# One transposing DMA for each moved unit, unit 24 moved, and two column sums on VectorE, in a graph layer kernel on one core

## The reference

```
h  = relu(layernorm(x));  support = act_quant(relu(act_quant(h) @ weight_quant(weight)))
x  = x + adj @ support                       # layer 0
h  = relu(layernorm(x))
S  = (adj + adj.T) / 2 + I;  d = rowsum(S) ** -0.5
x  = x + (adj @ (d[:, None] * S * d[None, :])) @ h    # layer 1
```

## Time and profile before

| | |
|---|---|
| median of 3 runs | 495.47 us (495.06 to 495.62) |
| the profiled execution's own time | 496.49 us |
| its span, first to last instruction | 494.7 us |
| TensorE busy | 478.1 us, 97% of the span |
| TensorE clock granted | 1.000 of full |
| transposing DMAs | 42, one for each half (high, low) of 21 moved units |

### The profile page before, as it was taken

How to read it: one execution, slowest core, us unless ns; L and a number is a source line. 1 busy time by engine, 2 the same in 40 slices (tenths; PEclk the granted TensorE clock), 3 DMA queues, 4 the chain that set the end, 5 groups by cost and what they waited for, 6 DMA issues and landing times.

```text
span 494.7 us, 6414 instructions
## 1 busy us (share of the span) xinstructions
PE 478.1 (97%) x2358; PEld 232.0 (47%) x2358; DVE 268.5 (54%) x360; ACT 154.1 (31%) x300; POOL 46.6 (9%) x54
## 2 busy tenths in 40 slices
PE   1899999999999999999999999999999999999997
PEld 1755544444454444444444444444444444444446
DVE  4966996779999688876997767340100001000010
ACT  1787833767562435344521121140000000000000
POOL 2320963213200000000000000000000000000000
PEclk9999999999999999999999999999999999999999
DMA  8986999999986242332232321045010000100001
GB/s 286 401 333 161 233 193 231 225 220 229 233 241 249 65 135 98 95 117 85 85 122 91 113 99 42 0 168 193 23 42 21 21 21 21 42 21 21 21 23 43
DMA packets 63180, 62.66 MB, mean 127 GB/s; under 512 B 46136, under 2 KB 46392, under 8 KB 63160
## 3 DMA queue, kind: packets, MB, share of 16 engines
q1 hardware_dynamic: 63152, 62.40, 44.3%
q10 hardware_dynamic: 8, 0.00, 0.0%
HBM read 42.99 MB, written 8.39 MB: 104 GB/s over the span
## 4 chain that ended last, share of the span: by engine, by line
PE 84%; DVE 8%; DMA 4%; SPq 2%; ACT 1%; issue 1%; POOL 0%; ACTq 0%
PE ps_a L1204 31%; PE ps_p L1102 13%; PE ps_p L1167 7%; PE ps_a L1167 7%; PE ps_b L1167 7%; PE ps_m L1167 4%; PE ps_h L1167 4%; DMA feat<-in_x 2%; PE ps_b L1053 1%; PE ps_m L1102 1%; PE ps_h L1102 1%; DVE at L763 1%; DVE small L944 1%; PE ps_b L1220 1%; PE ps_a L1220 1%; PE ps_a L1053 1%
## 5 line engine op out<-in xcount | busy, mean ns | idle before, releaser
L1102 PE MATMUL ps_p<-small,at 128*128 128x512 f16 x448 | 99.2, 379 | 0.4 <-DVE feat L884 0.4
L1022 DVE SCALAR_TENSOR_TENSOR feat<-ps_a,feat 128x512 f32<-128x512 f32 (+1 forms) x16 | 10.8, 675 | 148.7 <-PE ps_a L1204 144.2
L1204 PE MATMUL ps_a<-small,at 128*128 128x512 f16 x360 | 80.2, 379 | 0.0
L1204 PE MATMUL ps_a<-a_in,at 128*128 128x512 f16 x360 | 80.2, 379 | 0.0
L1102 PEld LDWEIGHTS ps_p<-small,at 128*128 128x128 f16 x448 | 43.7, 98 | 50.8 <-DVE feat L884 0.7
L584 ACT ACTIVATE split<-a_in 128x1024 f16<-128x1024 f32 x30 | 31.7, 1057 | 101.8 <-PE ps_p L1167 90.0
L940 DVE TENSOR_TENSOR split<-a_in,split 128x1024 f16<-128x1024 f32 x30 | 36.7, 1224 | 34.0 <-ACT split L584 34.0
L1204 PEld LDWEIGHTS ps_a<-small,at 128*128 (+1 forms) x360 | 35.2, 98 | 42.5
L1204 PEld LDWEIGHTS ps_a<-a_in,at 128*128 (+1 forms) x360 | 35.2, 98 | 42.5
L1167 PE MATMUL ps_p<-feat,split 128*128 (+1 forms) x180 | 43.9, 379 | 0.5 <-DVE small L944 0.5
L1167 PE MATMUL ps_a<-feat,split 128*128 (+1 forms) x180 | 43.8, 379 | 0.0
(11 more groups left out here) (182 smaller groups left out, 436.0 us busy)
## 6 DMA issues: line engine op xcount, KB each, us to landing
a_in<-in_adj SPq DMA_DIRECT2D x46, 512.0 KB, 3.9
at<-in_adj SPq DMA_DIRECT2D x16, 512.0 KB, 8.9
out<-feat SPq DMA_DIRECT2D x31, 256.0 KB, 4.3
feat<-in_x SPq DMA_DIRECT2D x8, 512.0 KB, 11.6
feat<-out SPq DMA_DIRECT2D x4, 1024.0 KB, 9.3
at<-in_L_gnn_weight SPq DMA_DIRECT2D x2, 512.0 KB, 4.0
at<-at SPq DMA_TRANSPOSE x42, 4.7
split<-in_adj SPq DMA_DIRECT2D x1, 512.0 KB, 15.7
```

Source lines behind the costliest of these rows:

```text
L1022: nc.vector.scalar_tensor_tensor(out, products, 1.0 / (SA * SZ), out, ALU.mult, ALU.add).then_inc(y_out, 1)
L1102: last = nc.tensor.matmul(l0_bank(r), at_block(r, lo, j), small[:, j * D:(j + 1) * D], start=(j == 0 and lo == 0), stop=(j == T - 1 and lo ...
L1204: last = nc.tensor.matmul(BANK[n], at_block(t, lo, j), z_part(j, z_lo), start=(j == 0 and lo + z_lo == 0), stop=(j == T - 1 and lo == 1))
```

## The change

- `EVEN` gets unit 24: it is no longer turned by TensorE but moved. Round 10 turns nothing; round 9 moves 23, 24 and 25.
- A moved unit is one transposing DMA of 128 x 2048 in place of two of 128 x 1024, and it starts when the low part is ready. For that `at` is laid out unit by unit: a unit's high and low halves are neighbours. There is one semaphore for each staging buffer.
- Since the halves of units 28 to 31 now lie elsewhere over the staging buffers, `hi_turned(28)` waits for unit 26 alone, `hi_turned(30)` for none, and `hi_turned(31)` for unit 29.
- The column sums of units 10 and 14 move from ScalarE to VectorE, at the ends of rounds 5 and 7; those of 18 to 26 stand in other rounds on ScalarE.
- The load of 28 is started behind the move of 24, that of 29 behind the move of 25 (before: both behind 25, 29 first).

```diff
-EVEN = (10, 12, 14, 18, 20, 22, 26)
+EVEN = (10, 12, 14, 18, 20, 22, 24, 26)
+SUMMED_LATE = (10, 14)
...
+        def staged(u):
+            k = stage_no(u)
+            return late(14 + k // 2, 2 * W * (k % 2 if k < 2 else 1), 2 * W, f16)
         def stage(u, lo):
+            return staged(u)[:, lo * W:(lo + 1) * W]
...
+        def at_half(u, lo):
+            return at[:, (2 * u + lo) * W:(2 * u + lo + 1) * W]
         def at_block(r, lo, j):
-            return at[:, ds(r * PAIR + lo * N + j * P, P)]
+            return at[:, ds(r * PAIR + j // B * 2 * W + lo * W + j % B * P, P)]
...
-                 9: [23, 25], 10: [26], 11: [27, 29]}
+                 9: [23, 24, 25], 10: [26], 11: [27, 29]}
-        SUMS_OF = {5: [[(10, FIRST)], [], [(10, LAST)]], 7: [[(12, FIRST)], [(12, LAST)], []],
-                   8: [[(14, FIRST)], [(14, LAST)], []], 9: [[(18, FIRST)], [(18, LAST)], []],
-                   10: [[], [], [(20, FIRST)]], 11: [[], [(20, LAST)], [(22, FIRST)]],
-                   12: [[], [], [(22, LAST), (26, FIRST)]], 13: [[], [], [(26, LAST)]]}
+        SUMS_OF = {7: [[(12, FIRST)], [(12, LAST)], []], 8: [[(18, FIRST)], [(18, LAST)], []],
+                   9: [[(20, FIRST)], [(20, LAST)], []], 10: [[(22, FIRST)], [], [(22, LAST)]],
+                   11: [[], [], [(24, FIRST), (24, LAST)]], 12: [[], [], [(26, FIRST), (26, LAST)]]}
...
             def move(u):
-                for lo, ready in ((0, hi_ready), (1, lo_ready)):
-                    sp.wait_ge(ready, MOVED.index(u) + 1)
-                    if u == 29:
-                        wait_moved(sp, MOVED[-3])
-                        wait_moved(sp, MOVED[-2])
-                    elif u >= 12:
-                        free_slot(waited_in(u)[lo])
-                    sp.dma_start_transpose(at_half(u // 2, lo, u % 2).rearrange("p (b i) -> p b i", i=P), stage(u, lo))\
-                      .then_inc(at_moved[stage_no(u)][lo], 16)
+                sp.wait_ge(lo_ready, MOVED.index(u) + 1)
+                if u == 29:
+                    wait_moved(sp, MOVED[-2])
+                elif u >= 12:
+                    free_slot(waited_in(u)[u % 2])
+                sp.dma_start_transpose(at_unit(u).rearrange("p (b i) -> p b i", i=P), staged(u))\
+                  .then_inc(at_moved[stage_no(u)], 16)
...
-                     23: [27], 25: [29, 28], 26: [30], 27: [31]}
+                     23: [27], 24: [28], 25: [29], 26: [30], 27: [31]}
...
                 if u == 28:
                     wait_moved(act, MOVED[-3])
-                    wait_moved(act, MOVED[-2])
-                elif u == 30:
-                    wait_moved(act, 29)
+                elif u == 31:
+                    wait_moved(act, MOVED[-1])
...
                 if r - 3 in LATE_SUMS:
                     column_sum_late(r - 3)
+                for k, u in enumerate(SUMMED_LATE):
+                    if r == (5, 7)[k]:
+                        wait_moved(dve, u)
+                        column_sum_late(u)
```

More of the change, by code:

```diff
@@ L26 @@
 LATE_SUMS = (0, 2)
-EVEN = (10, 12, 14, 18, 20, 22, 26)
-SUMMED = EVEN
+EVEN = (10, 12, 14, 18, 20, 22, 24, 26)
+SUMMED_LATE = (10, 14)
 MOVED = tuple(sorted(tuple(range(3, 30, 2)) + EVEN))
@@ L186, in gnn_kernel @@
         lo_ready = sem("lo_ready")
-        at_moved = [[sem(f"at_moved{k}{lo}") for lo in range(2)] for k in range(3)]
+        at_moved = [sem(f"at_moved{k}") for k in range(3)]
         atlo = sem("atlo")
@@ L209, in gnn_kernel @@
         feat3 = feat[:, :].rearrange("p (t d) -> p t d", d=D)
-        at4 = at[:, :].rearrange("p (r two i) -> p r two i", two=2, i=N)
+        at5 = at[:, :].rearrange("p (r h two i) -> p r h two i", h=2, two=2, i=W)
         def in_tile(u):
@@ L251, in part, with at_unit @@
             return split[:, (2 * k + lo) * W:(2 * k + lo + 1) * W]
-        def at_half(r, lo, h):
-            return at[:, r * PAIR + lo * N + h * W:r * PAIR + lo * N + (h + 1) * W]
+        def at_unit(u):
+            return at[:, u * 2 * W:(u + 1) * 2 * W]
+        def at_half(u, lo):
+            return at[:, (2 * u + lo) * W:(2 * u + lo + 1) * W]
         def at_block(r, lo, j):
-            return at[:, ds(r * PAIR + lo * N + j * P, P)]
+            return at[:, ds(r * PAIR + j // B * 2 * W + lo * W + j % B * P, P)]
         def at_across(h, lo, j):
-            return at4[:, B * h:B * (h + 1), lo, j * P:(j + 1) * P]
+            return at5[:, B * h:B * (h + 1), j // B, lo, j % B * P:(j % B + 1) * P]
         def g_part(t, lo):
@@ L300, in wait_moved @@
             same = [w for w in MOVED[:k + 1] if stage_no(w) == stage_no(u)]
-            for lo in range(2):
-                engine.wait_ge(at_moved[stage_no(u)][lo], 16 * len(same))
+            engine.wait_ge(at_moved[stage_no(u)], 16 * len(same))
         def arrivals(u):
@@ L490, in sum_blocks @@
                 wait_moved(act, u)
-                both = at4[:, u // 2, :, (u % 2) * W:(u % 2 + 1) * W].rearrange("p two (b i) -> p b two i", i=P)
+                both = at_unit(u).rearrange("p (two b i) -> p b two i", two=2, i=P)
                 if parts[0]:
@@ L519, in hi_turned @@
                         act.wait_ge(rs_done, TURNED.index(first) + 1)
-                nc.scalar.activation(at_half(u // 2, 0, u % 2), turn_bank(u)[:, :], ACT.Copy, scale=SA)\
+                nc.scalar.activation(at_half(u, 0), turn_bank(u)[:, :], ACT.Copy, scale=SA)\
                   .then_inc(athi, 1)
@@ L754, in lo_turned @@
                 dve.wait_ge(athi, TURNED.index(u) + 1)
[L755 to L759, removed]
+                nc.vector.scalar_tensor_tensor(at_half(u, 1), turn_bank(u)[:, :], SA, at_half(u, 0),
+                                               ALU.mult, ALU.subtract).then_inc(atlo, 1)
             def lo_rows(u):
@@ L971, in _ @@
             link(nc.vector.memset(pause[:, :], 0.0))
+            late_sums = colp[:, :].rearrange("p (u b) -> p u b", b=B)[:, SUMMED_LATE[0]:SUMMED_LATE[-1] + 1:4, :]
+            nc.vector.tensor_scalar(late_sums, late_sums, 1.0 / SA, None, ALU.mult)
             link(nc.vector.tensor_scalar(colp[:, a:b], colp[:, a:b], 1.0 / SA, None, ALU.mult))
@@ L978, in _ @@
             for moved_sums in (rs3[:, ADDED[1] // 2:ADDED[-1] // 2 + 1, 1],
-                               rs3[:, 5:14:2, 0], rs3[:, 6:11:4, 0]):
+                               rs3[:, 5:14:2, 0], rs3[:, 6, 0:1], rs3[:, 10:13:2, 0]):
                 last = nc.vector.tensor_scalar(moved_sums, moved_sums, 1.0 / SA, None, ALU.mult)
```

2 lines of the change are left out of this document (removed).

## The result

| | median us | runs | ratio to before, 95% interval |
|---|---|---|---|
| before | 495.47 | 495.06 to 495.73 | 1 |
| changed | 499.40 | 498.06 to 500.02 | 1.0077 [1.0064, 1.0091] |

The change makes the kernel 0.8% slower, 3.9 us, where 2.3 were forecast: the sign is as predicted and the time within the range, but the size is 1.6 us off. The profiled execution is the fastest of its six, 498.06 us with a span of 496.3.

The account below looks back on a forecast made before the run. TensorE's instruction stream was taken to set the time, its DMA queue nearly full. Gains of at most 2.5 us were outweighed by load 29's lateness: turn(30) at 139.2 against 136.92, +2.3 us on 495.5, so 497.8; range 494.2 to 500.0.

Parts of the forecast that it names:

- load of 27 lands: DMA queue: this load lands 0.2 us later than 119.73, with -0.9 and +1.1 as ends.
- load of 29 lands: DMA queue: this load lands at 128.7, 4.3 us later than before.
- wait before `turn("acc")`: TensorE, ready since 128.36, waits for GpSimd's addition of unit 29 until 131.1: a new wait of 2.7 us.
- The period of merged move and load: SyncE's queue: one load and one merged move take 4.40 us, against 4.50 before; its error counts five times.
- B: Faster: the merged DMA takes the stall out, period 3.3 us, all of 2.5 us won, 493.0 us; chance 0.25.
- C: No change within 1 us: merging saves 0.3 to 0.6 us a period, gain and new wait cancel, 495.5; chance 0.18.
- D: Much slower: the merged start stalls whole, period 5.7 us, 504 us; chance 0.06.
- Two periods to the load of 29: Queue: move 24, load 28 and move 25 lie between loads 27 and 29: two periods of 4.40 us, before one.
- The sums on VectorE: Column sums of 10 and 14, 2.27 us each; the one in round 5 makes round 6 about 1.1 us late.
- The 0.44 us before tile 12: TensorE's gap before tile 12 goes, since VectorE no longer reduces unit 24 (1.1 us) in round 10.
- The chain before `turn(30)`: From load 29 through ScalarE's two batches of sums (1.6 us each) and VectorE, to turn(30) at 139.2.
- A's upper case: Likeliest case (slower by 2.3 us, chance 0.51) with period 4.50 and VectorE's delay not hidden: 4 us, 499.5.

Follow-up runs that it names:

- e3: Changed kernel with load 29 issued before load 28, both behind the move of unit 24; 497.37 us, ratio 1.0042.
- e7: Changed kernel with the column sums of units 10 and 14 back on ScalarE; 498.90 us, ratio 1.0057.
- e5: Changed kernel with load 29 before load 28 and ScalarE's column sums of unit 24 behind unit 28's high part, 26's behind 30's; 495.00 us, ratio 0.9996.
- e2: Changed kernel with two transposing DMAs for each moved unit, each behind its own part, in the new layout; 499.62 us, ratio 1.0081.
- e6: Changed kernel with ten unused products on TensorE ahead of its wait for acc; 499.49 us, ratio 1.0069.
- e10: e6 plus eight unused products on TensorE into a free bank ahead of turn(30); 498.01 us, ratio 1.0061.
- e4: Changed kernel with ScalarE's column sums of unit 24 behind unit 28's high part, those of 26 behind 30's; loads as changed; 497.19 us, ratio 1.0028.
- e1: Kernel before with only the merged DMA and its layout; unit 24 turned on TensorE, loads and column sums as before; 494.30 us, ratio 0.9981.
- e11: Kernel before with the additions and split of sum tile 1 two rounds later, ScalarE's part with them; 493.88 us, ratio 0.9985.
- e8: e5 plus VectorE's additions of sum tile 1 moved from round 10 to 12 and their split from 11 to 13; 493.87 us, ratio 0.9956.

## Why the prediction came out as it did

On before's clock, by the prediction's steps:

| step | predicted | measured (+1.21) |
|---|---|---|
| load of 27 lands | 119.9 | 119.87 |
| load of 29 lands | 128.7 | 128.96 |
| addition of 29 done | 131.1 | 131.36 |
| wait before `turn("acc")` | 2.7 | 2.89 |
| `hi_turned(28)` | 134.0 | 134.36 |
| column sum of 28 | 136.75 | 137.23 |
| `turn(30)` | 139.2 | 139.70 |
| execution | +2.3 | +3.9 |

- **The period of merged move and load**, the number that counted five times, was right in the main: a merged start behind a load took 3.5 to 3.6 us in the five periods from the load of 25 to that of 30, against 3.5 to 3.8 for two halves in before, and nothing of the stall went away or doubled. Rivals B, C and D fall with it. The two periods from the load of 27 to that of 29 took 9.09 us for 8.8. The higher rate that the Trainium skill gives for contiguous sources (page "DMA: Bandwidth & Descriptors", section "Latency and other measured facts") did not shorten the period here by the 0.6 us estimated from it: 4.2 to 4.8 us between load starts with 4 KB in one piece, 4.2 to 4.6 in before with 2 KB.
- **Two periods to the load of 29**: right, and e3 proves it by taking one away.
- **The sums on VectorE**: `x1_tile(5)` was to start 1 us later; it started at 83.38, 0.94 later on before's clock. The load of 27 was put 0.2 us later, 1.1 for the sums less 0.9 for the merge. The sum came out (119.87 for 119.73), and so did its terms: without the sums e7 has this landing 1.07 us earlier, at 118.80 on before's clock, 0.9 before 119.73.
- **The 0.44 us before tile 12** went as forecast, but by luck. The reason given, one reduce less on VectorE, isn't enough: in e3 and e5, which have that reduce less too, the wait is 0.92 and 0.76. It went since the load of 29 came late. The last operation of sum tile 1, which runs beside GpSimd's addition of unit 29 in before, e3 and e5, was by itself in the changed kernel, and VectorE got to `x1_tile(10)` 2.0 us sooner on before's clock, all of it by this operation: it began sum tile 1 at the same time (120.46 and 120.39). Before and changed:

```profile
125.06 2.33 DVE L935 SCALAR_TENSOR_TENSOR tmp<-ident,tmp 128x128 f32<-128x128 f16 x1
```

```profile
123.91 0.29 DVE L933 SCALAR_TENSOR_TENSOR tmp<-ident,tmp 128x128 f32<-128x128 f16 x1
```

- **The chain before `turn(30)`**: 0.5 us longer than forecast. 0.26 is the load; the two batches of sums took from 128.81 to 132.20, 3.4 for 3.2.
- **A term that was left out: the clock.** The sum priced every instruction behind the new waits at its old duration. In the changed kernel TensorE stands for 2.9 us before `turn("acc")`, and where a second wait of 2 us follows, what comes after runs partly at the lower clock, 1.7 us longer (e2, e6 and e7, all three profiled in executions of 499.1 to 499.8). In the changed kernel's own profile the loss fell before the second wait and cost nothing; that execution had 498.06. All six had a granted clock of 0.996 or 0.997, the profile of before 1.000.
- **The rest of the 3.9 us stays open.** On before's clock the profiled execution is 2.8 us over before, 0.5 us more than forecast; 1.1 us are left to the 3.9 of the medians. The clock is one candidate, but the step isn't shown: no execution of the changed kernel with the loss on the path was profiled, and a remainder as large is left where the clock didn't fall. e10, at 1.000 in every run, takes 137.41 us from the front to layer 1 and before 135.22, 2.2 more, but 3.0 by its ratio; e5, at 0.999 or 1.000, takes 134.11, 1.1 less, but 0.2 less by its ratio. The one profile of before may simply be long in this stretch.
- **Slips in the sums**, none of which moves the forecast: 103.99 - 102.64 - 1.25 is 0.10, not 0.09. The fourth of the DMA digits is a 6. With periods of 4.50 and VectorE's delay in full, A's upper case comes to 119.73 + 1.1 + 9.0 = 129.8 for the load of 29, 3.4 us slower and not 4.
- **Where the loss comes from**: of the 3.9 us (0.8%), the order of the two loads accounts for 0.35% (e3), ScalarE's order for 0.49% (e4), and both together for all of it (e5). The merged DMA with its layout gains 0.2% (e1). The figures for e3 and e4 are differences of ratios whose intervals are about 0.3% wide.

## What to carry to other kernels

A step that moves from a full engine to a queue that is also nearly full is paid at the queue, and who pays is decided by what is next in it: one swapped pair of loads and one batch of sums put behind the step that TensorE waits for turned +0.8% into 0, and a third reordering into -0.4%. (That third one is worth 0.15% in the kernel before by itself, e11.) When two chains end near each other, compute each end at undisturbed durations; one profile may show one of them stretched by something that fills a wait. And when a change opens a wait on TensorE, price what follows it too, at the clock that the traces show behind such waits.

## What had not been expected of the hardware

- TensorE's clock fell behind waits of 2 to 3 us: 24 matmuls of 5.34 us took 7.03 behind one wait of 2.9 us, in other executions those were at full speed and 8 matmuls of 1.89 took 2.8 to 3.6 behind a later wait of 2.0 to 2.2. The whole loss was 1.7 us in each of the five traces that show it. With 2.4 and 1.95 us of unused products in the two waits (e10) the granted clock was 1.000 in all runs, and these runs differ by 0.35 us where those of the changed kernel differ by 2.0. In e4 a wait of 2.77 us with no second one left the profiled execution at full clock, though 8 of its 12 runs had 0.996 or 0.997: which execution is hit was not the same from run to run.
- VectorE's additions of 1.22 us took up to 3.43 beside GpSimd's of 2.4, which then took 2.9 to 3.4. The Trainium skill, page "SBUF — State Buffer", section "SBUF: two separate sides", says that a VectorE operation with two inputs in on-chip memory and a GpSimd operation exclude each other for a whole instruction. The trace of e5 agrees: VectorE's first addition, started at 120.12, ended 1.1 us behind GpSimd's (123.49 and 122.40), about its own length; with its place changed the same VectorE addition is back at 1.21 us (e8).
- The wait for the weight statistics near the start varied from 2.0 to 4.3 us between profiled executions of kernels that are alike there, and the end of the front with it from 22.2 to 24.5, which has to be taken out before two single profiles are compared.
